# A slot's gate and up products placed behind the down products of the slot six back

## What is computed

```
for each channel, over time t:   # the mixing layer, a scan along the 128 tokens
    y[t] = (exp(u + k[t]) * ctx[t] + P[t]) / (exp(u + k[t]) + Q[t])    # P, Q decay by exp(w), then add exp(k)*ctx and exp(k)
x = x + tanh(g1) * y                      # k = NORM(x), v = ctx
z = had(NORM(x) * SU_ug) / 64             # (1024 tokens) x 256
up   = z @ W_up.T   * (scale_up * 64)     # 256 -> 1024
gate = z @ W_gate.T * (scale_gate * 64)   # 256 -> 1024
h = had(silu(gate) * up * SU_dp) / 64
out = x + tanh(g2) * (h @ W_down.T * (scale_down * 64))   # 1024 -> 256
```

## Time and profile before

| | us |
|---|---|
| median of 3 runs | 107.75 |
| the runs | 107.71, 107.75, 108.75 |
| the profiled execution, its own time | 107.85 |
| span of its profile | 106.1 |

### The profile page before, as it was taken

One profiled execution on the slowest core, in us unless ns is written; L12 is line 12 of the kernel. 1 busy time (PEld: TensorE's weight loads), 2 busy tenths in 40 slices (PEclk: granted clock), 3 DMA queues, 4 the chain that ended last, 5 costly groups with the idle time before them and its releaser, 6 DMA issues.

```text
span 106.1 us, 2023 instructions
## 1 busy us (share of the span) xinstructions
PE 100.3 (95%) x724; PEld 91.1 (86%) x724; DVE 70.2 (66%) x150; ACT 68.0 (64%) x153; POOL 60.6 (57%) x73
## 2 busy tenths in 40 slices
PE   6999999989999999988999999799999999999990
PEld 5788788659666999978999999799999999999980
DVE  0398889899999996898998269942298231134221
ACT  4098967999939899924337997555976432442400
POOL 7025979993996995149996245355208234235500
PEclk9999999999999999999999999999999999999998
DMA  1889999400000000000000000020000200000202
GB/s 57 267 322 393 419 416 399 182 3 6 0 0 0 0 6 0 0 0 3 0 0 6 0 0 0 0 105 0 0 0 3 99 6 0 0 0 3 99 6 99
DMA packets 2893, 7.70 MB, mean 73 GB/s; under 512 B 321, under 2 KB 706, under 8 KB 2754
## 3 DMA queue, kind: packets, MB, share of 16 engines
q1 hardware_dynamic: 2882, 7.56, 18.9%
HBM read 6.51 MB, written 1.05 MB: 71 GB/s over the span
## 4 chain that ended last, share of the span: by engine, by line
PE 59%; ACT 17%; DVE 13%; issue 8%; DVEq 0%; POOL 0%; ACTq 0%; POOLq 0%
PE UG L964 25%; PE VB L837 6%; PE OD L1002 5%; PE FX L881 4%; PE VB L1002 3%; PE KZ L1002 3%; PE FX L1002 3%; ACT L564 2%; PE FX L927 2%; ACT L567 2%; DVE SQ L670 2%; PE OD L894 2%; PE VB L894 2%; PE KZ L894 2%; DVE H L814 2%
## 5 line engine op out<-in xcount | busy, mean ns | idle before, releaser
L484 POOL TENSOR_TENSOR HL<-H,HH 128x256 fp32r<-128x256 f32 x32 | 25.5, 803 | 28.5 <-ACT HH L623 28.4
L814 DVE SCALAR_TENSOR_TENSOR H<-S,ALPHA,UG 128x256 f32<-128x256 f32 x32 | 15.0, 477 | 16.7 <-ACT S L632 16.6
L632 ACT ACTIVATE S<-UG,HI 128x256 f32<-128x256 f32 x32 | 15.0, 471 | 13.6 <-PE UG L964 13.6
L964 PE MATMUL UG<-FH,WTH 128*128 128x256 f32 x128 | 21.7, 292 | 0.7 <-DVE H L814 0.5
L623 ACT ACTIVATE HH<-H 128x256 fp32r<-128x256 f32 x32 | 13.2, 414 | 11.3 <-DVE H L814 11.2
L964 PE MATMUL UG<-FL,WTH 128*128 128x256 f32 x128 | 20.0, 279 | 0.0
L964 PE MATMUL UG<-FH,WTL 128*128 128x256 f32 x128 | 19.8, 277 | 0.0
L964 PEld LDWEIGHTS UG<-FH,WTH 128*128 128x128 f32 x128 | 17.5, 188 | 2.4 <-issue 1.5
L964 PEld LDWEIGHTS UG<-FL,WTH 128*128 128x128 f32 x128 | 17.0, 188 | 0.2
L964 PEld LDWEIGHTS UG<-FH,WTL 128*128 128x128 f32 x128 | 17.0, 188 | 0.0
L837 PE MATMUL VB<-ONES 128*128 128x256 f32 x32 | 10.2, 483 | 1.0 <-POOL ONES L438 1.0
(11 more groups left out here) (158 smaller groups left out, 218.5 us busy)
## 6 DMA issues: line engine op xcount, KB each, us to landing
WN<-in_weights SPq DMA_DIRECT2D x4, 512.0 KB, 9.2
DN<-in_w_down SPq DMA_DIRECT2D x1, 1024.0 KB, 6.8
out<-XT SPq DMA_DIRECT2D x3, 256.0 KB, 2.5
X<-in_x SPq DMA_DIRECT2D x2, 256.0 KB, 4.0
V<-in_ct SPq DMA_DIRECT2D x2, 256.0 KB, 7.7
XT<-in_xt SPq DMA_DIRECT2D x2, 256.0 KB, 9.3
X<-in_x SPq DMA_DIRECT2D x1, 512.0 KB, 9.2
V<-in_ct SPq DMA_DIRECT2D x1, 512.0 KB, 11.5
```

What stands on the lines that cost most here:

```text
L484: pool.tensor_tensor(HL[:, q % JT, 0:n], ring(H, q), HH[:, q % JT, 0:n].bitcast(F32), ALU.subtract).then_inc(h_lo, 1)
L632: act.activation(ring(S, q), gate_part(q), ACT.Silu, scale=VT[:, V_SGATE + j:V_SGATE + j + 1]).then_inc(silu_ready, 1)
L814: dve.scalar_tensor_tensor(out=ring(H, q), in0=ring(S, q), scalar=ALPHA[:, j:j + 1], in1=up_part(q), op0=ALU.mult, op1=ALU.mult).then_inc( ...
L964: return pe.matmul(dst.rearrange("p (g n) -> p g n", n=GT), w[:, m, j, t, :], f[:, chunks, t, :], start=start, stop=stop, skip_group_check ...
```

## The change

In the loop that orders TensorE's work the call of `down(q - LAG)` is put ahead of `up(q)` instead of behind it. It acts for slots 6 to 31, since `down` is called there only from slot 6 on. The entries of PE_STAGES stay at the end of the slot's turn, and the tail is as it was. No instruction is added or dropped, and no other engine's program is touched.

```diff
             for q in range(-1, SLOTS):
+                if q >= LAG:
+                    down(q - LAG)
                 if q >= 0:
                     up(q)
-                if q >= LAG:
-                    down(q - LAG)
                 for name, g in PE_STAGES.get(q, []):
                     stage(name, g)
```

## The result

The changed kernel takes 109.88 us in the median (109.81 to 109.95, 4 runs); the kernel before, run beside it, 108.25 (107.71 to 109.05, 4 runs). The ratio is 1.0162, interval 1.0103 to 1.0222: slower. The forecast was slower with 109.05 us and a range of 108.3 to 109.4; the time lies above the range.

A forecast was written before the change was run, and what follows sets the result against it. TensorE's own queue was taken to bound the kernel behind 35 us; 0 up to 69.91, 0.65 at the ones matmul and 0.65 in the tail took 107.75 to 109.05 us, range 108.3 to 109.4.

The forecast's parts named there:

- The early part nets 0: Up to 69.91 us: D's fill the holes ahead of U9 and U16, but waits for XL and XH return it; 0.
- The ones matmul, 0.65 us: Group 3's ones matmul, near 74 us: a new wait for FSUM plus restart, 0.65 us from a range of 0.56 to 0.80.
- The chain S, HH, HL, FSUM: Behind U18: S of slot 18, HH and HL of slot 17, then FSUM, each 0.68 us later.
- the way from GpSimd: Delay from FSUM's end on GpSimd to TensorE's ones matmul, taken as 0.05 to at most 0.17 us.
- The tail, 0.65 us: First half of D30, near 101 us: a new wait for HL of slot 30 plus restart, 0.65 us (0.54 to 0.78).
- D31's half: In the tail: its HL is there at 101.55 us, the half moves to about 102.37, so it waits for nothing.
- The sum, 1.3 us: Whole kernel: 0 up to 69.91 us, 0.65 at the ones matmul, 0.65 in the tail; 1.1 to 1.6 by bounds.
- From there on all blocks run back to back, so nothing gives the time back: Behind the ones matmul of group 3: FH and FL are covered by over 3 us, so its 0.65 us delay stays.
- The restart: After each new wait TensorE's first four matmuls take 0.12 us more; nothing if weight loads were pulled ahead.
- The rivals: Four other outcomes: one wait only (chance 0.17), gains kept (0.05), no change (0.05), slower still (0.08).
- Slower still: Later FSUM meets a long VectorE operation and takes 1.7 instead of 0.74 us, adding 1.0: 110.0 us; chance 0.08.

The follow-up runs named there:

- the sum early: Kernel before with GpSimd's sum of group 3 in slot 16 instead of 17, nothing else; 1 of 11 executions in the lower group (107.87 us).
- the filled version: Kernel before with new order for slots 6 to 18, transforms of groups 2 and 3 and group 2's ones matmul a slot later; 106.63 us, ratio 0.9854.

## Why the prediction was wrong

- *The early part nets 0*: right, to 0.01 us in two traces that start alike, and by the run with only that part changed (0.9994, and 32.31 us of the stretch against 32.35 and 32.33).
- *The ones matmul, 0.65 us*: right. Its block starts 0.70 us later; taking the wait away gave 0.64 back in the medians and 0.57 in the traces. The chain S, HH, HL, FSUM moved as told, and the way from GpSimd was 0.15 us.
- *The tail, 0.65 us*: right, 0.60 between the traces of the two kernels; D31's half did not wait.
- *The sum, 1.3 us*: the step that failed is "From there on all blocks run back to back, so nothing gives the time back". It took for granted that back to back means 0.68 us for a D and 1.36 for a U throughout. TensorE has a second pace, 4% slower at the same granted clock, and between the two waits the changed kernel had it, which is the missing 1.0 us: 0.99 between the traces of the two kernels, and 1.04 between two without either wait. The waits themselves came to 1.2 us by the traces, so the forecast was short by a term that it put at nothing, not by those it named. The trace of the kernel before shows this pace too, between the ones matmul of group 2 and the transform of group 3, where the wait for XH hid it; the sum gives it no term.
- The one run of three at 108.75 was the other sign. It was taken for noise of a run; it is most likely the kernel before at the slow pace. Against that group the loss is 1.0 us, against the other 2.1 to 2.2. With the slow pace on both sides the traces, which leave out the head, give 35.31 - 34.13 = 1.2 us.
- *The restart*, 0.12 us forecast: 0.11 measured in the tail. Weight loads were not pulled ahead over a wait here: the load of the waiting matmul of D30 starts with it at 102.26, while in the stream a load starts 0.11 us ahead of its matmul.
- The rivals: none of them was this. "Slower still" had the right side and another mechanism; FSUM took 0.73 us, as before.

What is shown: the two waits and their prices, the two paces, that the pace can change at the ones matmul of group 3 without a wait or a gap, with the old order as with the new, and that a stop can bring the quick one back. Nearly shown: that the upper group of the kernel before is the slow pace. No trace of that kernel itself in that group was taken, but three with its order behind slot 17 were (109.34 us; 108.78 with the sum early; 108.83 with the ones matmul behind U20), and each is slow behind its ones matmul, with 34.04 to 34.13 us where the two quick traces have 33.03 and 33.05. Open: what in TensorE or its queue sets the pace, why the early sum goes with the slow one, whether the format of the ones matmul shifts the odds, why the changed kernel, which does stop there, had the slow one, by the times and three traces, in 16 of 16 executions (with those of slot 31 in the old order) while the filled version, which stops there too, was quick in four of six, and why the share differs by chip.

## What to carry to other kernels

Where a block is moved past another on the bounding engine, price both sides of every value that passes between the engines: the holes it fills are worth something only if the next late value comes earlier too, and each consumer with less slack than the moved block's length (here 0.17 and 0.19 against 0.68 us) becomes a wait. Read the distance from matmul to matmul in each stretch, not only the waits, and take the time between two marks in the traces where the whole time holds a head that varies. When a kernel's own runs fall into groups, find the groups' cause before forecasting a difference of their size.

## What the hardware showed that was not expected

- The fp32r stream of weight load and 128x256 matmul ran at 0.1133 or 0.1178 us from matmul to matmul at a granted clock of 1.00, each for tens of matmuls. It changed at stops, at ones matmuls with or without a gap, and once across a transform (0.1178 ahead, 0.1133 behind, nothing late).
- The Trainium skill (TensorE: Matmul & The Clock Gate, Back-to-back issue gap) gives N / 2.4 + 2.5 ns for an isolated matmul at the full clock, an estimate of 0.109 us for 256 columns, and says that in a stream of weight loads and matmuls the spacing is set by both, with about 81 ns for 128 columns and 131 ns for 512. The stream here has 0.113 or 0.118 us for 256 columns: between those two, and 4% or 8% above the isolated one.
- An added stop made a kernel no slower or a little faster, since the quick pace behind it was worth more than the stop.
